# Projecting one batch before attention and the other three inside its steps

## What is computed

```python
def bitnet_linear(x, weight, scale_param):
    s = max(mean(abs(weight), axis=1), 1e-08)
    y = einsum('bsi,oi->bso', x, sign(weight / s[:, None])) * (s * scale_param)
    return nan_to_num(y, nan=0.0, posinf=1e6, neginf=-1e6)

h = layernorm(x)
q, k, v = (bitnet_linear(h, w, c) for w, c in (q_, k_, v_))     # 32, 8 and 8 heads of 16 channels
attn = softmax(q @ k.T / 4)                                       # each key head serves 4 query heads
x = x + bitnet_linear(attn @ v, o_weight, o_scale)
W = base + mean(abs(w - base)) * sign(w - base)                   # for w1, w2, w3
x = x + (silu(h2 @ W1.T) * (h2 @ W3.T)) @ W2.T                    # h2 = layernorm(x)
```

## Time and profile before

| | |
|---|---|
| median of three runs | 1074.68 us (1073.73 to 1074.82) |
| profiled execution | 1078.31 us, span 1076.5 us |
| TensorE matmuls busy | 955.0 us, 89% of the span |
| Vector busy | 784.5 us, 73% |
| Scalar busy | 528.8 us, 49% |
| GpSimd busy | 132.8 us, 12% |
| mean granted TensorE clock | 0.948 of 2.4 GHz |

### The profile page before, as it was taken

How to read it: one execution, slowest core, us unless ns; L and a number is a source line. 1 busy time by engine, 2 the same in 40 slices (tenths; PEclk the granted TensorE clock), 3 DMA queues, 4 the chain that set the end, 5 groups by cost and what they waited for, 6 DMA issues and landing times.

```text
span 1076.5 us, 14793 instructions
## 1 busy us (share of the span) xinstructions
PE 955.0 (89%) x4770; PEld 624.1 (58%) x4770; DVE 784.5 (73%) x1088; ACT 528.8 (49%) x972; POOL 132.8 (12%) x150
## 2 busy tenths in 40 slices
PE   1838348999999999997968999999999999999997
PEld 0727313333333333332445888888888888888886
DVE  6847468999999999996796557864588456864443
ACT  3624206888888888886556332232313332132221
POOL 0204001122111211110000111101101011011110
PEclk9978758999999999997889999999999999999999
DMA  7134324555456544634457200231002400040001
GB/s 253 35 101 164 117 100 122 179 147 145 131 168 170 140 142 143 183 80 142 138 159 238 68 1 1 66 114 60 0 0 78 161 0 0 9 147 1 0 0 39
DMA packets 78962, 106.06 MB, mean 99 GB/s; under 512 B 12960, under 2 KB 36512, under 8 KB 78912
## 3 DMA queue, kind: packets, MB, share of 16 engines
q1 hardware_dynamic: 75360, 101.04, 30.7%
q10 hardware_dynamic: 2688, 2.63, 0.7%
q0 software_dynamic: 864, 1.77, 0.5%
HBM read 76.29 MB, written 28.58 MB: 97 GB/s over the span
## 4 chain that ended last, share of the span: by engine, by line
PE 63%; DVE 14%; SPq 9%; DMA 8%; issue 4%; ACT 1%; POOL 0%; DVEq 0%; ACTq 0%
PE psum L1219 14%; PE psum L1220 14%; PE psum L1221 14%; DVE nmx L861 8%; PE psum L1133 6%; SPq L371 6%; PE psum L1123 6%; PE psum L1107 4%; DMA x_sb<-_attn_hidden_states_dram 2%; DMA factors<-wstat 2%; DVE dsum L947 2%; DMA q_parts<-q_lo 1%; PE psum L1144 1%; PE psum L1209 1%; PE psum L1145 1%
## 5 line engine op out<-in xcount | busy, mean ns | idle before, releaser
L687 ACT ACTIVATE probs<-psum 128x512 f32<-128x512 f32 x512 | 274.3, 602 | 92.5 <-PE psum L1123 91.5
L861 DVE TENSOR_REDUCE nmx<-psum 128x2 f32<-128x1024 f32 x256 | 300.4, 1218 | 26.3 <-PE psum L1107 24.2
L1219 PE MATMUL psum<-fxh,wh 128*128 128x512 f32 x448 | 175.2, 391 | 2.2 <-DVE wl L993 2.2
L1123 PE MATMUL psum<-q_slot,k_slot 50*128 50x512 f32 x512 | 160.4, 488 | 17.0 <-DMA q_slot<-shift 10.0
L1220 PE MATMUL psum<-fxl,wh 128*128 128x512 f32 x448 | 175.0, 391 | 0.0
L1221 PE MATMUL psum<-fxh,wl 128*128 128x512 f32 x448 | 174.8, 390 | 0.0
L1123 PEld LDWEIGHTS psum<-q_slot,k_slot 50*128 50x128 f32 x512 | 78.0, 190 | 135.5 <-ACT probs L687 101.1
L1133 PE MATMUL psum<-probs,v_slot 128*32 128x512 f32 x1024 | 140.7, 622 | 3.0 <-ACT probs L687 0.7
L1000 DVE TENSOR_TENSOR gate<-gate,psum 128x512 f32<-128x512 f32 x56 | 38.4, 686 | 133.8 <-PE psum L1221 131.5
L1107 PE MATMUL psum<-k_slot,q_slot 48*128 48x512 f32 x512 | 114.6, 460 | 9.6 <-DVE nmx L861 6.6
L745 ACT ACTIVATE hh<-gate 128x512 fp32r<-128x512 f32 x56 | 35.4, 632 | 162.6 <-DVE gate L1000 162.6
(11 more groups left out here) (102 smaller groups left out, 1148.1 us busy)
## 6 DMA issues: line engine op xcount, KB each, us to landing
stage<-in_L_ffn_mean_w_dram SPq DMA_DIRECT2D x84, 256.0 KB, 4.5
q_slot<-q_parts SPq DMA_DIRECT2D x174, 64.0 KB, 2.9
stage<-in_L_ffn_w_dram SPq DMA_DIRECT2D x42, 256.0 KB, 3.1
weighted_values<-u_sb SPq DMA_DIRECT2D x32, 256.0 KB, 2.2
k_slot<-k_stack SPq DMA_DIRECT2D x58, 96.0 KB, 2.7
x_sb<-_attn_hidden_states_dram SPq DMA_DIRECT2D x4, 1024.0 KB, 14.6
q_parts<-q_hi SPq DMA_DIRECT2D x32, 128.0 KB
q_parts<-q_lo SPq DMA_DIRECT2D x32, 128.0 KB
```

What stands on the lines that cost most here:

```text
L687: nc.scalar.activation(probs[kt][:, j, :], BANK[ring_bank(("score", g, kt, j))], ACT.Exp, scale=HEAD_DIM ** -0.5).then_inc(exp_ok, 1)
L861: v.tensor_reduce(column, pair, AX.X, ALU.max, negate=True).then_inc(s_max, 1)
L1123: mm(BANK[ring_bank(("score", g, kt, j))], k_slot[s][rows, kt * P:(kt + 1) * P], q_slot[s][rows, jj, :], start=True, stop=True).then_inc(t ...
L1219: mm(o, lhs_hi, rhs_hi, start=first, stop=False)
```

## The change

Only batch 0 is projected up front. The six projections of a later batch (ITEMS: k, four of q, v) are done inside the 32 attention steps of the batch before it, at fixed steps: statistics on Vector in steps 0 to 4, norm on GpSimd in step 5, one transposed token tile in each of steps 8 to 11, one item in each of steps 13, 15, 17, 19, 21 and 23, the transpose of values in step 28. On TensorE such a tile is the last of its step, after the fourth shifted score; it is a user of the ring of three banks, and Scalar evacuates it after the exps of the step. Behind the evacuation, GpSimd splits the tokens (steps 9 to 12), guards an item one step later and splits it four steps later, after Vector's selection in that same step. SP stores an item at the start of the group of its step plus six.

Other edits that come with it: only one batch of tokens is on chip at a time; q is stored as a stack of three parts (high, high, low), so a group's queries are loaded by two DMAs in place of six, and an item is stored by three DMAs of 256 KB; the first groups are loaded by SP; the output weights are loaded by SP and their signs taken after batch 0's values; the factors of the output projection are written and waited for by SP behind the loads of group 2 and ahead of the first shift; the copy of u on Scalar now comes ahead of the exp of s3; the sums of magnitudes move from Vector to Scalar (Abs) and GpSimd (an addition into dacc of 1536 columns), with one final reduction of dacc on Vector; the scaled tile yq has a ring of two in place of four; the loops of the first stage are written out.

The diff, cut to its core. STATS_AT and the like are steps within a batch, the LAGs are steps after an item's or difference's own step. norm_tokens does four TENSOR_SCALAR of 512 columns on GpSimd; guard_item does two on GpSimd and select_item one COPY_PREDICATED on Vector.

```diff
+ITEMS = (KTILE, QT, QT + 1, QT + 2, QT + 3, VTILE)
+SLICES = KV_HEADS * TT
+STATS_AT, AGGR_AT, NORM_AT, XT_AT, SPLIT_AT = 0, 4, 5, 8, 9
+ITEM_AT = tuple(13 + 2 * i for i in range(len(ITEMS)))
+GUARD_LAG, PRED_LAG = 1, 4
+VT_AT = 28
+DIFF_AT = tuple(range(1, 112, 8))
+SIGN_LAG, ABS_LAG, SUM_LAG = 2, 5, 8
+Q_RING = 3
...
-Y_RING = 4
+Y_RING = 2
...
-    q_dram = nc.dram_tensor("q_parts", [GROUPS, 2, HEAD_DIM, REP, SEQ], FP32, kind="Internal").ap()
+    q_dram = nc.dram_tensor("q_stack", [GROUPS, REP, ROWS, SEQ], FP32, kind="Internal").ap()
...
+    def beside(g, kt):
+        b, at = g // KV_HEADS + 1, 4 * (g % KV_HEADS) + kt
+        if b == BATCH:
+            return None
+        if XT_AT <= at < XT_AT + KT:
+            return "xT", b, at - XT_AT
+        if at in ITEM_AT:
+            return "item", b, ITEM_AT.index(at)
+        if at == VT_AT:
+            return "vT", b
+        return None
...
     def load_group(eng, g, s, done):
         for h in range(2):
-            rows = q_slot[s][HALF * h:HALF * h + ROWS].bitcast(FP32)
-            parts = q_dram[g, :, :, 2 * h:2 * h + 2, :]
-            for copy in range(2):
-                eng.dma_start(rows[HEAD_DIM * copy:HEAD_DIM * (copy + 1)], parts[0]).then_inc(done, 16)
-            eng.dma_start(rows[2 * HEAD_DIM:ROWS], parts[1]).then_inc(done, 16)
+            eng.dma_start(q_slot[s][HALF * h:HALF * h + ROWS].bitcast(FP32),
+                          q_dram[g, 2 * h:2 * h + 2].rearrange("j r t -> r j t")).then_inc(done, 16)
             eng.dma_start(k_slot[s][HALF * h:HALF * h + ROWS].bitcast(FP32), k_dram[g]).then_inc(done, 16)
...
+        load_tokens(0)
+        sp.wait_ge(w_in[1], 32)
+        sp.dma_start(w_nat[:, OT:, :], o_w.rearrange("(t p) c -> p t c", p=P)).then_inc(w_in[2], 16)
+        sp.wait_ge(xT_ok, KT)
+        load_tokens(1)
+        store_item(0, 0)
+        store_item(0, 1)
+        sp.wait_ge(slot_init, 10)
+        for g in range(2):
+            group_stored(g)
+            load_group(sp, g, g, slot_in[g])
+        store_item(0, 2)
+        store_item(0, 3)
+        store_item(0, 4)
+        group_stored(2)
+        load_group(sp, 2, 2, slot_in[2])
...
+        def sp_group(g):
+            b, at = divmod(4 * g, SLICES)
+            first, last = g == 0, g >= GROUPS - 4
+            s = g % 4
+            if b + 1 < BATCH:
+                for i in range(5):
+                    if at <= ITEM_AT[i] + 6 < at + 4:
+                        store_item(b + 1, i)
+            if g + 3 < GROUPS:
+                positive(sp, t_mm, 16 * g)
+                group_stored(g + 3)
+                load_group(sp, g + 3, (s + 3) % 4, slot_in[(s + 3) % 4])
+            if g < LAST_G:
+                load_shift(g + 1, (s + 1) % 4)
+            for e in range(2, IT):
+                if 4 * g - 2 < DIFF_AT[e - 2] + SUM_LAG + 1 <= 4 * g + 2:
+                    load_difference(e)
+            if b + 2 < BATCH and at == XT_AT + 4:
+                sp.wait_ge(xT_ok, KT * (b + 2))
+                load_tokens(b + 2)
...
+        def split_tokens(b, kt):
+            pool.wait_ge(xe_ok, 4 * (b - 1) + kt + 1)
+            if kt == 0:
+                pool.wait_ge(q_mm, NI * b)
+            nc.gpsimd.tensor_copy(xh[:, kt, :], xT[kt % 2][:]).then_inc(xh_ok, 1)
+            pool.wait_ge(xh_ok, 4 * b + kt + 1)
+            nc.gpsimd.tensor_tensor(xl[:, kt, :], xT[kt % 2][:], xh[:, kt, :].bitcast(FP32), ALU.subtract).then_inc(xl_ok, 1)
+        def guard_item(b, i):
+            n, m = NI * b + i, ITEMS[i]
+            y, alt, mask = yq[n % 2][:], g_alt[n % 2][:], g_mask[n % 2][:]
+            pool.wait_ge(yq_ok, n + 1)
+            if i == 1:
+                pool.wait_ge(vT_mm, b)
+            else:
+                pool.wait_ge(ql_ok, 5 * b + (i - 1 if i else 0))
+            nc.gpsimd.tensor_scalar(alt, y, GUARD, -GUARD, ALU.min, ALU.max).then_inc(mask_ok, 1)
+            nc.gpsimd.tensor_scalar(mask, y, wstat[:, 4, m:m + 1], 0.0, ALU.mult, ALU.is_equal).then_inc(mask_ok, 1)
+        def split_item(b, i):
+            c, n = 5 * b + i, NI * b + i
+            pool.wait_ge(yg_ok, n + 1)
+            if c >= Q_RING:
+                pool.wait_ge(part_out[c % Q_RING], STORES * (c // Q_RING))
+            nc.gpsimd.tensor_copy(q_hi[c % Q_RING][:], g_alt[n % 2][:]).then_inc(qh_ok, 1)
+            pool.wait_ge(qh_ok, c + 1)
+            nc.gpsimd.tensor_tensor(q_lo[c % Q_RING][:], g_alt[n % 2][:], q_hi[c % Q_RING][:].bitcast(FP32), ALU.subtract
+                                    ).then_inc(ql_ok, 1)
...
+        def add_magnitude(e):
+            pool.wait_ge(fabs_ok, 3 * (e + 1))
+            positive(pool, facc_ok, e)
+            nc.gpsimd.tensor_tensor(dacc[:], dacc[:], mn[e % 2][:], ALU.add).then_inc(facc_ok, 1)
...
+        def pool_slice(g, kt):
+            b, at = g // KV_HEADS, 4 * (g % KV_HEADS) + kt
+            if kt == 1 and 0 < g < LAST_G:
+                pool.wait_ge(pv_mm, 4 * g)
+                if (g + 1) % KV_HEADS == 0:
+                    pool.wait_ge(v_ok, (g + 1) // KV_HEADS + 1)
+                fill_values(g + 1)
+            if b + 1 < BATCH:
+                if at == NORM_AT:
+                    norm_tokens(b + 1)
+                if SPLIT_AT <= at < SPLIT_AT + KT:
+                    split_tokens(b + 1, at - SPLIT_AT)
+                for i in range(NI):
+                    if at == ITEM_AT[i] + GUARD_LAG:
+                        guard_item(b + 1, i)
+                    if at == ITEM_AT[i] + PRED_LAG and i < 5:
+                        split_item(b + 1, i)
+            for e in range(IT):
+                if 4 * g + kt == DIFF_AT[e]:
+                    difference(e)
+                if 4 * g + kt == DIFF_AT[e] + SUM_LAG:
+                    add_magnitude(e)
...
+        def beside_out(user):
+            kind, b, *which = user
+            bank = ring_bank(user)
+            if kind == "xT":
+                kt = which[0]
+                act.wait_ge(xT_ok, 4 * b + kt + 1)
+                if kt >= 2:
+                    act.wait_ge(xl_ok, 4 * b + kt - 1)
+                elif b > 1:
+                    act.wait_ge(xl_ok, 4 * b + kt - 1)
+                nc.scalar.activation(xT[kt % 2][:], BANK[bank], ACT.Copy).then_inc(xe_ok, 1)
+            elif kind == "item":
+                scale_item(b, which[0], bank)
+            else:
+                values_out(b, bank)
...
+        def act_slice(g, kt):
+            for j in J_ORDER:
+                if j == J_ORDER[3]:
+                    if kt == 0 and g > 0:
+                        copy_u(g - 1)
+                act.wait_ge(t_mm, score_number(g, kt, j) + 1)
+                if j == 0:
+                    positive(act, pv_mm, 4 * g + kt - 3)
+                nc.scalar.activation(probs[kt][:, j, :], BANK[ring_bank(("score", g, kt, j))], ACT.Exp,
+                                     scale=HEAD_DIM ** -0.5).then_inc(exp_ok, 1)
+            if beside(g, kt):
+                beside_out(beside(g, kt))
+            if g >= GROUPS - 4 and (g % 4, kt) == SPLIT_STEP:
+                for k in range(KT):
+                    hi_attended(0, k)
+            for e in range(IT):
+                k = 4 * g + kt - DIFF_AT[e] - SIGN_LAG
+                if 0 <= k < 3:
+                    act.wait_ge(fd_ok, e + 1)
+                    nc.scalar.activation(sgn[:, e, k, :], wn[e % 2][:, k, :], ACT.Sign).then_inc(fsgn_ok, 1)
+                if 3 <= k < 6:
+                    nc.scalar.activation(mn[e % 2][:, k - 3, :], wn[e % 2][:, k - 3, :], ACT.Abs).then_inc(fabs_ok, 1)
...
+        def select_item(b, i):
+            n = NI * b + i
+            dve.wait_ge(mask_ok, 2 * n + 2)
+            settle(dve)
+            v.copy_predicated(g_alt[n % 2][:], g_mask[n % 2][:], yq[n % 2][:]).then_inc(yg_ok, 1)
...
-            v.tensor_reduce(dtot[:], dsum[:], AX.X, ALU.add).then_inc(dtot_ok, 1)
+            dve.wait_ge(facc_ok, IT)
+            v.tensor_reduce(dtot[:], dacc[:], AX.X, ALU.add).then_inc(dtot_ok, 1)
...
+        def dve_slice(g, kt):
+            b, at = g // KV_HEADS, 4 * (g % KV_HEADS) + kt
+            n = 8 * g + 2 * kt + S_AHEAD
+            for a in range(2):
+                if n + a < S_USES:
+                    maxima(n + a)
+                if a == 0 and b + 1 < BATCH:
+                    if STATS_AT <= at < STATS_AT + TT:
+                        token_stats(b + 1, at - STATS_AT)
+                    if at == AGGR_AT:
+                        token_means(b + 1)
+                    for i in range(NI):
+                        if at == ITEM_AT[i] + PRED_LAG:
+                            select_item(b + 1, i)
...
+        def project_item(b, i, bank):
+            m = ITEMS[i]
+            w = slice(m * P, (m + 1) * P)
+            for kt in range(KT):
+                mm(BANK[bank], signs[:, kt, w], xh[:, kt, :], start=(kt == 0), stop=False)
+                last = mm(BANK[bank], signs[:, kt, w], xl[:, kt, :], start=False, stop=(kt == KT - 1))
+            last.then_inc(q_mm, 1)
```

(74 more changed lines are left out.)

615 lines of the change are left out of this document (267 added, 348 removed).

## The result

The changed kernel took 1096.65 us (median of 4 runs, 1092.02 to 1099.5) against 1074.2 for the kernel before on the same chip (1071.39 to 1074.82): a ratio of 1.0184, 95% interval 1.0146 to 1.0221. It is 22 us slower by the medians and 20 by the ratio; the forecast was 1055 us, 20 us faster. The profiled execution took 1097.69 us with a span of 1095.9. Two executions behind, one of e3_mask_vector (1334 us) and one of the kernel before (1492 us), ran at a granted clock of 0.65 and 0.56 throughout, and nothing is compared with them.

The account below looks back on a forecast made before the run. Sync-queue stores end the first stage; attention is a TensorE-Scalar loop with Vector nearly as full. Against 91.5 us won stood 46.2 + 5 + 1.5 + 4.5 + 10.5 + 2 + 2 = 71.7, so 1074.7 becomes 1055 us, range 1030 to 1078.

Parts of the forecast that it names:

- start: First stage, now one batch: the first shifted score comes at 72 us instead of 163.5, a gain of 91.5 us.
- tiles (Part 2): Projections inside attention steps: 18 items at 1.9 us net and 15 transposed tiles at 0.8 cost 46.2 us.
- TensorE idle: Vector, reduction, GpSimd, shift, loads, selection: Attention delays from other engines and the sync queue, in that order: 5, 1.5, 4.5, 10.5, 2 and 2 us.
- the sum of Parts 2 and 3: Cost in attention of the tiles plus the delays from other engines and queues: 71.7 us, against 91.5 won.
- The forecast's own sign of being wrong: Attention above 468 us, pointing to slow GpSimd TENSOR_SCALAR or selections, or a first shifted score after 80 us.
- Rival D: Start gated longer by stores at 1.1 us and a slow factors write; first score at 80, 1063 to 1071 us; chance 0.15.
- The shift: Sync queue in group 6: item 4's store and loads delay the next shift, 3.5 us per batch, 10.5 in all.
- The other terms of Part 3: Attention: Vector work beyond its slack 5 us, weight-tile loads between first and second shift 2, selections slowed beside GpSimd 2.
- B: Attention: tiles stretch steps so queue and GpSimd keep up; about 50 us paid, 1033 us in all; chance 0.25.
- C: Steps 14 to 27: GpSimd becomes the bound if TENSOR_SCALAR takes 2.0 us; 1074.7 to 1088 us; chance 0.13.
- the upper bound I named: Vector's selection beside GpSimd: one can grow by up to 3.5 us, a whole GpSimd operation ahead of it.
- the second figure: Selections on Vector, by the skill's lock rule in step 19: up to 2 us per batch, 6 in place of 2.

Follow-up runs that it names:

- e3_mask_vector: Changed kernel with the mask of each later item (batches 1 to 3) computed on Vector instead of GpSimd: 1102.52 us (ratio 1.0257 to the kernel before).
- e4: Changed kernel with the extra tile after the third shifted score, ahead of PV, instead of last in its step: 1083.98 us (1.0080).
- e7: Changed kernel with 12 and 24 unread matmuls ahead of the waits for the shift at steps 24 and 28: 1080.5 us (1.0060).
- e2: Changed kernel with the factors' write behind the first shift and their read in the sync queue's third group: 1101.01 us (1.0226).
- e12: As e11, with factors moved as in e2, the first two differences' loads behind group 1's shift, and the first difference at step 3: 1090.53 us (1.0133).
- e8: Changed kernel writing one row instead of 128 per later item store, later batches loading batch 0's operands (work left out): 1071.71 us (0.9971).
- e5: Changed kernel with items 0, 2, 3 and 4 stored behind the loads and shift of their groups, item 1 still ahead: 1080.94 us (1.0058).
- e13: Changed kernel, tile mid-step, stores behind loads and shift, items 0, 1 selected and split three steps behind their matmuls, stored at step 16: 1074.26 us (1.0004).
- e14: As e13, with GpSimd's weight difference ahead of the addition of magnitudes in a step that has both: 1076.86 us (0.9989).
- e16: As e14, with the weight difference's loads moved from the group of step 24 to that of step 28, behind its shift: 1085.79 us (1.0089).
- e1: Changed kernel with the next group's shift issued ahead of the item stores and loads in every sync-queue group: 1111.92 us (1.0345).
- e9: Changed kernel, tile mid-step, items 0, 2, 3, 4 stored behind loads and shift, step 20's shift ahead of item 1's store and loads: 1086.94 us (1.0102).
- e11: As e9, with the weight difference that starts at step 25 of a batch set to start at step 28: 1091.82 us (1.0164).

## Why the prediction was wrong

In its own steps, first PV to last PV for "attention":

| term | predicted | measured |
|---|---|---|
| start | -91.5 | first shifted score 163.5 to 78.9: -84.6 |
| tiles (Part 2), busy time | 46.2 | about 47 |
| TensorE idle: Vector, reduction, GpSimd, shift, loads, selection | 25.5 | +29.1 |
| TensorE's clock, busy time | no term | about 28 |
| sum | -20 | +20.1 at the last PV |

**The step that failed is the sum of Parts 2 and 3: it prices every stall by its own length and every matmul at full speed.** The trace shows 104.1 us where 71.7 were forecast, and the granted clock fell from 0.96 to 0.89 over attention. Busy time grew by 75.0 us. The tiles' own part is 47, counted below at full clock; the rest is 28, and 77 us more at 1.2 GHz at e4's 0.38 us each give 29. That the clock is what was missing is shown twice: e4 runs the same matmuls with 22.6 us less of busy time, and e7 leaves the queue alone, fills the idle time ahead of the shift with matmuls that nobody reads, and gains 13 us. The forecast's own sign of being wrong came true (473.6 us of attention, above 468), but it pointed at GpSimd's operations and at the selections, and not at the clock.

**The start.** The mechanism was right: SP waits for the factors' landing just ahead of the first shift. The term was 7 us too large, since the nine stores ended at 57.6, not between 47 and 53: they began at 47.4 instead of 43 and took 1.13 us each. The factors made up for a part, with a landing of 13.3 us instead of 16.6. Rival D gave 80 for the first score and named the stores; the slow factors write that it also named was not there. e2 and e12 show that the first group was not worth more anyway: the 12 and 10 us won there were gone by the second group and by step 12.

**The tiles.** Nearly right. The PV rows of three items and three plain steps, 266.14 to 289.52:

```profile
266.14 1.07 PE L1272 MATMUL psum<-probs,v_slot 128*32 128x512 f32 x8
271.11 1.06 PE L1272 MATMUL psum<-probs,v_slot 128*32 128x512 f32 x8
273.72 1.06 PE L1272 MATMUL psum<-probs,v_slot 128*32 128x512 f32 x8
...
289.52 1.06 PE L1272 MATMUL psum<-probs,v_slot 128*32 128x512 f32 x8
```

A step with an item takes 4.97 us, one without 2.61. The six take 23.38, and six steps of before (2.74 each) 16.4: 2.3 per item, against 1.9 predicted. A transposed tile is some 0.65 against 0.8. 18 x 2.3 + 15 x 0.65 = 51, with the idle time inside these steps. TensorE's busy time alone, at full clock, in the steps of batch 1 that hold tiles against the same steps of before: 44.1 us against 31.8 for six items, 13.5 against 10.7 for four token tiles, so 2.1 and 0.7 each, 47 in all.

**The waits.** Scalar's token copies wait 5.0 us in 3 for GpSimd, 4.5 predicted. The shift was mis-sized: 26.1 us in place of 10.5. The place was right, the sizes not: step 28 waits 5.2 to 5.3 us where 3 were counted, step 24 2.0 to 2.7 and step 20 about 1 where 0 to 1 were. The loads behind the stores take 3.8 us of the queue, and the stores' landing was nowhere in the count: ahead of step 24 the last store of item 1 has been issued at 282.5 and the loads that need it go at 287.9. e8, which takes the landings away and leaves the rest, and e5, which takes the stores from in front, both leave 6 us of these 26. The other terms of Part 3 (Vector 5, loads 2, selection 2) did not appear as idle time of that size, so the idle sum is near by cancelling, not by being right.

**The rivals.** B (late chains vanish) fell: the tiles' slack does not reach steps 24 to 28. C gave the right side for the wrong reason. GpSimd's TENSOR_SCALAR does take 2.00 us with a scalar of each partition, the end that C named, but only in one of the two operations of a guard; six guards take 16 us and not C's 24. (C also counted twelve steps with six items, 42.6 us of TensorE; its steps 14 to 27 are fourteen with five items, 45.9 at the same prices.)

```profile
L646 POOL TENSOR_SCALAR g_mask<-yq,wstat 128x512 int32<-128x512 f32 x18 | 36.0, 2002 | 1.7
...
L645 POOL TENSOR_SCALAR g_alt<-yq 128x512 f32<-128x512 f32 x18 | 12.0, 668 | 41.1 <-ACT yq L759 40.3 <-POOL q_lo L656 0.5
```

but GpSimd is busy for 72 of 118.5 us in a batch, and e3, with the masks gone from it, is no faster. A selection held for up to 3.5 us by GpSimd, the upper bound I named, was seen (3.94 in e5). In the changed kernel the longest are the three of step 19, the step that the prediction named, one in each batch:

```profile
274.04 2.40 DVE L956 COPY_PREDICATED g_alt<-g_mask,yq 128x512 f32<-128x512 int32 x1
```

```profile
272.36 3.47 POOL L662 TENSOR_TENSOR stage<-stage 128x1536 f32<-128x1536 f32 x1
```

The mean of all 24 is 0.995 us, so together they take 6 us more than at 0.74 each. That is the second figure that the prediction gave for them, where it took 2.

**What stays open.** With the shift in time (e13) the change breaks even: first PV comes 84.6 us sooner and attention takes back 78.9, of which 53 are busy time, mostly the tiles' own, and 26 idle; the few microseconds between them do not show in the medians, since the kernel before was profiled in an execution 3.6 us above its median. e14 and e16 each removed the idle stretch that they aimed at and got one at the next dependency. Of the 45 idle microseconds of e13, 38 are waits for Scalar's exponentials and Vector's maxima, and no run takes these apart. Whether a schedule exists in which nothing is handed on, and the change gains, was not found. What makes the clock fall after some idle stretches and not others (1.5 us at 246.0 and 2.65 at 293.1 in the changed kernel had no drop behind them, 1.5 us at 120.6 had), and why it comes back sooner in e4, is open too.

## What to carry to other kernels

When work is moved beside an engine that was 95% busy, split its stretch into busy time and idle time, and compare busy time for the same count of instructions: what grows without more work is here the clock, a second price of a stall. Reordering a queue that is late moved the wait to another place in e1, e9, e14 and e16, and helped only where what went behind was not needed yet (the stores in e5); what also helped was to bring the producing step forward (e13) or to shorten what must land (e8). And a gain at the start is worth only what the next dependency lets through (e2, e12).

## What the runs showed of the hardware

In the changed kernel TensorE's granted clock went to 1.2 GHz behind some idle stretches of 1.5 to 5.3 us, in stretches that were otherwise full, and came back after 3.4 to 17 us; behind others, up to 2.65 us long, it stayed. A PV takes 1.93 us at that level against 1.06, each microsecond there cost 0.38 us over attention (e4 against the changed kernel), and matmuls nobody reads, 0.25 us each, kept the clock up (e7).

A Vector selection of 0.73 us took 2.40 in the changed kernel and up to 3.94 in e5, and a Vector TENSOR_SCALAR of 128x4 took 2.60 instead of 0.17 in e11, each beside a GpSimd TENSOR_TENSOR of some 3.45 us; the selections ended 0.6 us after it, the small operation with it. The Trainium skill, SBUF — State Buffer, section Who interferes with whom, has this as a lock on the ports that the two engines share, taken by Vector instructions with two SBUF inputs and by some forms of copy, cast and tensor_scalar. The selections' rows agree; the small operation's agrees if it runs in such a form, which no run here shows. I had counted only the selections, so e11 moved the wait from one victim to the other.

GpSimd's TENSOR_SCALAR on 128x512 takes 0.67 us with two constants and 2.00 to 2.07 with one or two scalars for each partition; its conversion takes 0.61. The Trainium skill, GPSIMD Engine Reference, section 3.1, gives 0.77 us for such a loop with one input: near the 0.67 and the 0.61, and little more than a third of the 2.00.
